# A gathered convolution on one core: tile steps taken two by two, and the weighing moved inside them

## The reference, cut to what matters

```
pos  = clip(l + phase + freq * taps, 0, L - 1)        # 32 taps per token and head
g    = x[floor(pos)] + frac * (x[floor(pos)+1] - x[floor(pos)])
bins = clip(floor((offs + 256) / 512 * 64), 0, 63)
y    = einsum(kmat[bins], g);  x = x + ga * (y @ out_w.T)
```

## Time and profile before

| | |
|---|---|
| median of 3 runs | 1327.14 us (1326.66 to 1328.32) |
| the profiled execution | 1334.1 us |
| its span | 1332.0 us |
| busy: PE, PEld | 1143.9 us, 743.6 us |
| busy: DVE, ACT, POOL | 859.9 us, 788.1 us, 588.7 us |
| granted TensorE clock, mean | 0.955 of full speed |

### The profile page before, as it was taken

The page is one execution under the profiler, slowest core; times in us unless marked ns, Lnnn a source line. Parts: engine busy times, 40 slices in busy tenths (PEclk is TensorE's granted clock), DMA queues, the critical chain, the costliest instruction groups (busy, mean ns, idle before and its releaser), DMA issues. The chain is left out here.

```text
span 1332.0 us, 34891 instructions
## 1 busy us (share of the span) xinstructions
PE 1143.9 (86%) x11855; PEld 743.6 (56%) x11855; DVE 859.9 (65%) x2508; ACT 788.1 (59%) x1650; POOL 588.7 (44%) x838
## 2 busy tenths in 40 slices
PE   4699999999999999999999999999923989999840
PEld 2366656666666666666666666666611556565520
DVE  4477777787787778778777867777661333333336
ACT  2476676677667667766766776676501555555520
POOL 4233155346337435634733562442436545544520
PEclk9999999999999999999999999999956999999975
DMA  5546456446545544655654554544412442222237
GB/s 179 157 124 175 109 151 167 122 133 185 139 129 174 157 120 137 183 139 135 176 148 119 159 146 127 144 139 116 153 63 70 143 128 69 73 69 73 67 144 256
DMA packets 213179, 179.82 MB, mean 135 GB/s; under 512 B 147600, under 2 KB 183184, under 8 KB 212368
## 3 DMA queue, kind: packets, MB, share of 16 engines
q1 hardware_dynamic: 204336, 159.68, 43.3%
q0 software_dynamic: 8672, 17.92, 4.1%
HBM read 95.42 MB, written 82.12 MB: 133 GB/s over the span
## 5 line engine op out<-in xcount | busy, mean ns | idle before, releaser
L1325 DVE SCALAR_TENSOR_TENSOR aw<-ps,ks 128x64 f32<-128x64 f32 (+7 forms) x960 | 379.9, 435 | 207.8 <-PE ps L1015 170.6
L794 ACT ACTIVATE ps<-ps,f 128x512 f32<-128x512 f32 x512 | 342.4, 669 | 233.5 <-PE ps L1006 233.4
L1021 PE MATMUL ps<-ident,aw 128*128 128x128 f32 x2048 | 335.0, 287 | 36.2 <-ACT att L802 15.5
L1021 PEld LDWEIGHTS ps<-ident,aw 128*128 128x128 f32 x2048 | 217.3, 142 | 163.3 <-issue 124.5
L623 POOL COPY kn<-kn 128x256 f32<-128x256 f32 x64 | 25.5, 398 | 425.4 <-DVE kn L1309 425.4
L1011 PE MATMUL ps<-cn,ptt 32*128 32x512 bf16 x512 | 199.3, 389 | 3.5 <-ACT ps L794 3.5
L1015 PE MATMUL ps<-cn,ptt 32*128 32x512 bf16 x512 | 199.2, 389 | 0.0
L1006 PE MATMUL ps<-cp,ptt 32*128 32x512 bf16 x512 | 198.4, 390 | 0.0
L1335 DVE COPY att<-ps 128x512 f32<-128x512 f32 x256 | 175.7, 686 | 20.1 <-PE ps L1021 13.8
L724 POOL DMA_INDIRECT y_scratch<-aw,idu x135 | 129.3, 958 | 129.7 <-ACT aw L886 128.5
L802 ACT ACTIVATE att<-ps 128x512 f32<-128x512 f32 x256 | 151.8, 593 | 14.3 <-PE ps L1021 14.2
(11 more groups left out here) (177 smaller groups left out, 1695.8 us busy)
## 6 DMA issues: line engine op xcount, KB each, us to landing
k_scratch<-kn SPq DMA_DIRECT2D x64, 512.0 KB, 4.1
ka<-e_scratch SPq DMA_DIRECT2D x64, 512.0 KB, 3.4
ks<-k_scratch SPq DMA_DIRECT2D x128, 130.0 KB
e_scratch<-kr SPq DMA_DIRECT2D x128, 126.0 KB, 3.4
dl<-slot_scratch SPq DMA_DIRECT2D x135, 65.0 KB, 1.8
att<-y_scratch SPq DMA_DIRECT2D x16, 512.0 KB, 5.2
xc<-in_x SPq DMA_DIRECT2D x8, 512.0 KB, 6.3
h_scratch<-hx SPq DMA_DIRECT2D x16, 256.0 KB, 4.3
```

Source lines behind the costliest of these rows:

```text
L794: act.activation(ps_s[T % BANKS][:, :], ps_s[T % BANKS][:, :], ACT.Relu, scale=f27[:, i % 2, r, h:h + 1]).then_inc(s_e, 1)
L1021: last = nc.tensor.transpose(bank[:, j * P:j * P + P], aw[:, T % RING, j * P:j * P + P], ident[:, :])
L1325: ins = nc.vector.scalar_tensor_tensor(dst[:, a:b, :], src[:, a:b, :], -TAPS * SCALE, rows(ks[:, R % 2, h, o:o + 1], [[0, b - a], [1, HP]] ...
```

## The change

TensorE takes the tiles in twos. At even h it issues tile_on for T+2 and T+3, gap_on for T+4 and T+5, undone_on for T+2 and T+3, then, at h = 2 and h = 6, `weigh`, then turn_tile(T); at odd h it issues turn_tile(T) alone. `aw` becomes a ring of 4. ScalarE's lead over the turns grows from 3 to 4 tiles, so that it runs gap(T+4), tile_evicted(T), gap(T+5). VectorE weights two tiles ahead, and at odd T it runs tile_evicted(T) and then weighted(T+2). The count moves from h = 0 to h = 1, the edge turns from h = 2 and 4 to h = 3 and 5, behind `bins`.

```
--- before.py
+++ after.py
@@ -20,7 +20,7 @@
 ROWS = 32
 QUAD = P // ROWS
 KRING = 4
-RING = 3
+RING = 4
 BANKS = 4
 SCALE = 2.0 ** 27
 GATE = 2.0 ** 90
@@ -45,11 +45,11 @@
     for T in range(NT):
         i, R, r, h = T // TILES, T // HEADS, T // HEADS % RES, T % HEADS
         order.append(("tile", T))
-        if h == 0 and R + 1 < NR:
+        if h == 1 and R + 1 < NR:
             order.append(("count", R + 1))
-        if h == 2:
+        if h == 3:
             order.append(("edge", R, 0))
-        if h == 4:
+        if h == 5:
             order.append(("edge", R, 1))
         if h >= 6 and r == 3 and i:
             order.append(("h2", i - 1, h - 6))
@@ -822,24 +822,24 @@
             for n in range(4):
                 params_turned(0, n)
             counted(0)
-            for T in range(BANKS - 1):
+            for T in range(BANKS):
                 gap(T)
             for b in range(2):
                 steps_turned(0, b)
             for T in range(NT):
                 i, R, r, h = T // TILES, T // HEADS, T // HEADS % RES, T % HEADS
                 last, more = i - 1, i + 1 < PAIRS
-                if T + BANKS - 1 < NT:
-                    gap(T + BANKS - 1)
+                if T + BANKS < NT:
+                    gap(T + BANKS)
                 if h % 2 == 0:
                     tile_evicted(T)
-                if h == 0 and R + 1 < NR:
+                if h == 1 and R + 1 < NR:
                     counted(R + 1)
-                if h == 2:
+                if h == 3:
                     edge_evicted(R, 0)
                 if h == 3 and R:
                     copied(R - 1)
-                if h == 4:
+                if h == 5:
                     edge_evicted(R, 1)
                 if i:
                     if (r, h) in ((2, 1), (2, 3)):
@@ -1092,35 +1092,38 @@
             for n in range(4):
                 params_turned(0, n)
             counts(0)
-            for T in range(BANKS - 1):
+            for T in range(BANKS):
                 gap_on(T)
-            tile_on(0)
-            undone_on(0)
-            tile_on(1)
+            for T in range(2):
+                tile_on(T)
+            for T in range(2):
+                undone_on(T)
             for b in range(2):
                 steps_turned(0, b)
             for T in range(NT):
                 i, R, r, h = T // TILES, T // HEADS, T // HEADS % RES, T % HEADS
                 last, more = i - 1, i + 1 < PAIRS
-                if T + 1 < NT:
-                    undone_on(T + 1)
-                if T + 2 < NT:
+                if h % 2 == 0 and T + 2 < NT:
                     tile_on(T + 2)
-                if T + BANKS - 1 < NT:
-                    gap_on(T + BANKS - 1)
+                    tile_on(T + 3)
+                    if T + BANKS < NT:
+                        gap_on(T + BANKS)
+                        gap_on(T + BANKS + 1)
+                    undone_on(T + 2)
+                    undone_on(T + 3)
+                if h == 2 and R:
+                    weigh(R - 1, 1)
+                if h == 6:
+                    weigh(R, 0)
                 turn_tile(T)
-                if h == 0 and R + 1 < NR:
+                if h == 1 and R + 1 < NR:
                     counts(R + 1)
-                if h == 1 and R:
-                    weigh(R - 1, 1)
-                if h == 2:
-                    turn_edges(R, 0)
                 if h == 3 and R + 2 < NR:
                     bins(R + 2)
-                if h == 4:
+                if h == 3:
+                    turn_edges(R, 0)
+                if h == 5:
                     turn_edges(R, 1)
-                if h == 5:
-                    weigh(R, 0)
                 if h == 7:
                     weigh_edges(R, 0)
                     weigh_edges(R, 1)
@@ -1382,12 +1385,15 @@
             binned(0)
             binned(1)
             edge_terms(0)
+            for T in range(2):
+                weighted(T)
             for T in range(NT):
                 i, R, r, h = T // TILES, T // HEADS, T // HEADS % RES, T % HEADS
                 last, more = i - 1, i + 1 < PAIRS
-                weighted(T)
-                if T and h % 2 == 0:
-                    tile_evicted(T - 1)
+                if h % 2:
+                    tile_evicted(T)
+                if T + 2 < NT:
+                    weighted(T + 2)
                 if h == 2 and R + 1 < NR:
                     edge_terms(R + 1)
                 if h == 5 and R + 2 < NR:
@@ -1426,7 +1432,6 @@
                     new_x(i, 0)
                 if (r, h) == (7, 5):
                     second_spread(i, 0)
-            tile_evicted(NT - 1)
             i = PAIRS - 1
             new_x(i, 1)
             second_spread(i, 1)
```

## The result

The changed kernel takes 1453.26 us (median, 1443.53 to 1457.49) against 1327.73 for the kernel before in the same runs: a ratio of 1.093, 95% interval 1.087 to 1.099, so 126 us slower. The forecast was 1430, in a range of 1362 to 1463. The profiled execution spans 1455.5 us, against 1332.0.

What follows compares the result with a forecast made beforehand. TensorE bound the old kernel; a ring through VectorE would bound the new. Eight residues: 8 x 13.65 + 20.0 = 129.2 us against 115.06; six pairs +14.1, two +10.5, start -3: +103, so 1430 us, range 1362 to 1463.

Steps and rivals of the forecast that it cites:

- The ring through VectorE: Tile loop: next strips wait for turn T+1, VectorE's eviction and weighting; 2.82 us per two tiles, 3.83 with the weighing.
- the signs: Profile marks expected: strips' wait for VectorE becomes TensorE's longest, plain residue 13.3 to 13.7 us, odd turn to gap_on 2.1.
- The plain residue: Residue without side work, count to count: 13.65 us, at least 13.30, against 12.70 before.
- The late strips: Pair h = 2, 3 and the pair after: tile_on's strips aren't hidden, adding 0.17 and 0.18 us.
- The side work: Products, transposes, centring and VectorE's steps in eight residues: 20.0 us instead of 13.46.
- the centring: ScalarE's centring at h = 3 lies ahead of the ramp: twice 1.8 = 3.6 us in eight residues.
- The sum: Whole kernel: six pairs at +14.1, two at +10.5, the start at -3, together +103 us.
- rival 2: Tile loop: the ring is there but side work finds room in it, unchanged; 1365 to 1388 us, chance 0.2.
- The drain (rival 1): TensorE's strip groups: fewer drains decide and the kernel gets faster, 0.7 to 1.7 us per plain residue, 1218 to 1282; chance 0.07.
- Rival 4: Tile loop: it cancels, waiting gives back just what fewer strip groups save, 1327 us; chance 0.03.
- Rival 3: TensorE's gaps of 1.0 us or more in each pair take its clock to 1.2 GHz: 1550 us and up, chance 0.05.
- ScalarE's ring: Turn T, ScalarE's eviction and ramp, then tile_on's strips: 2.56 us, hidden behind 2.82 except in two places.

Runs made afterwards that it cites:

- the second experiment: Changed kernel with the second half of both centrings on ScalarE moved from h = 3 to h = 5: 1410.32 us, ratio 1.059.
- the third: Changed kernel with side transposes and their evictions both behind turn 7, instead of one behind turn 6 and one behind turn 7: 1431.27 us, ratio 1.076.
- The first experiment: Changed kernel with two VectorE lines exchanged: at odd T weighted(T+2) runs first, tile_evicted(T) behind it: 1338.71 us, ratio 1.006.

## Why the prediction was right, and where it was off

**The ring through VectorE was right**, in its place, its members and its length: 2.86 us for 2.82, and 3.81 for 3.83 with the weighing. Taking it away gave back 115 of 126 us. From an odd turn's load to the next gap_on there are 694.12 - 692.01 = 2.11 us, as the signs had it. One sign didn't come as told: the strips' wait for VectorE was to become TensorE's longest, with hundreds of microseconds. From 40 to 960 us it is 94.7 us on the loads of L1006, in 152 waits, and the edge turn's 97.0 is ahead of it. Only the second L1006 of a group waits, and in the group where TensorE's own work fills the ring, hardly at all.

**The plain residue** was 13.65, of which 0.35 were two places where the tile_on strips come late. Measured are 13.32, which is the bare ring of 13.30. The late strips exist (0.22 apart), but the two terms of 0.17 and 0.18 came as 3.88 - 3.83 = 0.05 and 2.86 - 2.82 = 0.04, and the other two pairs make 13.32 - 2.86 - 3.88 = 6.58 where 6.65 stood. So the step that prices the two places was too dear, 0.33 x 64 = 21 us; which overlap took the rest out wasn't tried.

**The side work** of eight residues was 20.0, measured 133.11 - 8 x 13.32 = 26.6. The step that failed is the clock. I set its chance at 0.05 and thought of it as all or nothing, the lower level through the whole loop. It comes in between: four of eight residues have 0.82 to 0.91. Residues 3 and 4 cost 4.4 us less at clock 1.00 in the second experiment, residue 2 costs 1.6 less at clock 1.00 in the third, and residue 1, at the same 0.90, is put at 1.6 too: together 7.6 us in eight residues, for which the sum had nothing. Against that the centring, 3.6 in the sum, comes to about 1.3 by the same rows (2.27 + 2.23 - 2 x 1.6). The remaining 6.6 - 7.6 + 2.3 = 1.3 us aren't assigned. In the six pairs of the middle the clock comes to some 6 x 7.6 = 46 us, an estimate.

Where the clock falls shows in the timeline of the changed kernel:

```profile
588.51 1.76 ACT L754 ACTIVATE hx<-xc,shift,rstd 128x128 f32<-128x128 f32 x4
...
591.39 0.42 PEld L1028 LDWEIGHTS ps<-ident,ka 128*128 128x128 f32 x4 [2.34 <-issue]
...
592.60 1.48 PEld L1042 LDWEIGHTS ps<-att,dl 128*32 128x32 f32 x32 [0.52 <-issue]
...
594.47 1.47 PEld L1021 LDWEIGHTS ps<-ident,aw 128*128 128x128 f32 x8 [0.38 <-issue]
...
596.11 0.44 PEld L1052 LDWEIGHTS ps<-att,hgr 128*32 128x32 f32 x16 [0.17 <-issue]
```

The edge turn waits 2.34 us for its bank, whose eviction stands behind the centring on ScalarE, so TensorE stands. Behind it the weighing's loads take 1.48 us instead of the 0.81 of the earlier trace rows, and eight turn loads 1.47 instead of 0.86: the lower level (1.2 GHz). At 596.11 the loads are at 0.44 again. The Trainium skill, "TensorE: Matmul & The Clock Gate", under "HAM oscillation", tells of a loop that waits for transfers in every round and pays this drop each time. The trace agrees that the drop comes again in each pair (four of its eight residues at 0.82 to 0.91); it differs in the waits, which are for an eviction and 2.3 us at the most.

But that wait doesn't settle it. The first experiment's kernel has it too, and keeps its clock:

```profile
534.17 0.42 PEld L1028 LDWEIGHTS ps<-ident,ka 128*128 128x128 f32 x4 [2.35 <-issue]
...
535.30 0.81 PEld L1042 LDWEIGHTS ps<-att,dl 128*32 128x32 f32 x32 [0.42 <-issue]
```

And in residues 3 and 4 of the changed kernel the clock falls where TensorE's waits are 1.2 us at most, while in the second experiment the same residues pass at 1.00 in one pair and fall in another. What decides whether it falls isn't shown. The runs show that from 300 to 840 us it is 0.94 with the ring, 1.00 with the exchange and 0.99 in the kernel before.

**The sum** came out at +103 for +126 because two errors have opposite signs: the late strips 21 us too dear, the side work 6.6 us too cheap in each of some seven groups of eight residues, 46 us. That the total came so close owes something to this luck. The lower end of the range, 1362, was called rival 2's, which is 1365. The interval of the runs lies above the forecast, so the miss of 23 us is real.

**The rivals.** The drain (rival 1) is out as the deciding term. With the exchange a plain residue takes 12.40 us, 0.30 less than before, with four strip groups instead of eight; that is far from the 0.7 to 1.7 that I gave it, and no run tells how much of it is the groups and how much the other moves of the edit. Rival 2, side work unchanged in the gaps, is out: 26.6 against 13.46. Rival 4 is out. Rival 3 holds in part, as told: the clock falls, but not at the price of 1550. The row it went by, the edge turn at 53.36, was read as the lower level from the loads' length alone; the granted clock of that place (53.3 to 54.1 us) reads 1.00, so the row doesn't show the level.

**ScalarE's ring** was too long by my count: 12.8 expected with the exchange, 12.4 measured. In its timeline strips to strips are 2.74 us for the pair h = 4, 5 (503.56 to 506.30) and 3.45 with the weighing (506.30 to 509.75), where I had 3.0 and 3.57.

## What to carry to other kernels

When an engine's loop is taken in twos, write down for each queue which instruction stands between "the result is ready" and "the next group may start", and add one period along it; here an eviction ahead of a weighting, two lines, was worth 115 us, while each engine's busy time said that there was room. A ring that leaves the bounding engine idle can cost twice on TensorE: here the granted clock was 0.94 with it and 1.00 without, so leave room for that in the range even where no single wait is long. Work put "to cover" another engine has to be placed anew when the ring changes: the same products gained 42 us behind the second turn while the ring stood, and lost 15 on another chip once it was gone.

## What the runs showed of the hardware that I had not expected

- TensorE's granted clock falls in a loop in which it is busy for 87% of the time, with no wait of TensorE over 2.3 us between 300 and 840 us: from 590.9 to 596.9 us the granted clock is 0.72. The same wait of 2.3 us in the kernel with the exchange was not followed by a fall. In the second kernel of the experiments the same residue took 16.37 us in one pair and 17.98 in another, by the clock alone.
- The kernel before took 1327 to 1334 us in the result's runs and on the first chip, and 1403 and 1408 us (medians) on two others, with pauses of ScalarE and VectorE, up to 3.5 us in its own profile there, that the profile gives to no instruction of this core.
- Strips of 32 rows and 512 columns on the same rows of the array start 0.23 us apart where nothing else holds them; on different rows within 0.01.
